# Masks of the first attention scores: from TensorE products to a fused VectorE add-and-maximum

## The reference, cut to what matters

```python
h = shift_token(x)
q, k, v = split(h @ wqkv)                      # 8 heads of 64
q, k = rotary_xpos(l2norm(q) * qs, l2norm(k) * ksc)
sim = einsum('bhwid,bhwjd->bhwij', bq, bk)     # windows of 128 queries, 256 keys
mask = (i < j) | (i > j + WINDOW) | (j == -1)
sim = where(mask, -finfo.max, sim)
attn = softmax(sim, axis=-1)
x = x + (attn @ bv) @ wo
h = layernorm(shift_token(x)) * lg + lb
a, g = split(h @ w1 + b1)
x = x + (a * gelu(g)) @ w2 + b2
```

## Time and profile before

| | us |
|---|---|
| median of 3 runs | 4159.85 (4159.74 to 4161.44) |
| profiled execution, its own time | 4161.62 |
| its span | 4159.9 |
| busy: PE, PEld | 3578.2, 2115.6 |
| busy: DVE | 2682.2 |
| busy: ACT | 2142.1 |
| busy: POOL | 1476.1 |
| mean granted TensorE clock | 0.946 |

### The profile page before, as it was taken

The page is one execution under the profiler, slowest core; times in us unless marked ns, Lnnn a source line. Parts: engine busy times, 40 slices in busy tenths (PEclk is TensorE's granted clock), DMA queues, the critical chain, the costliest instruction groups (busy, mean ns, idle before and its releaser), DMA issues.

```text
span 4159.9 us, 74766 instructions
## 1 busy us (share of the span) xinstructions
PE 3578.2 (86%) x26976; PEld 2115.6 (51%) x26976; DVE 2682.2 (64%) x4386; ACT 2142.1 (51%) x2586; POOL 1476.1 (35%) x1468
## 2 busy tenths in 40 slices
PE   2778788778775689999999999948899999999999
PEld 1222222222222456766676667625576667666666
DVE  4767667677673467667766776535766776676664
ACT  1555545555553345555555555424455555555564
POOL 1100101101001434544454555223454455445543
PEclk7999989999997789999999999978999999999999
DMA  2221211222212000110011001120011001100101
GB/s 48 36 47 41 48 36 40 52 41 38 45 36 68 6 21 23 33 34 24 23 33 35 23 23 37 32 68 14 14 33 35 23 23 33 35 23 30 36 21 34
DMA packets 149353, 139.79 MB, mean 34 GB/s; under 512 B 11420, under 2 KB 147664, under 8 KB 149200
## 3 DMA queue, kind: packets, MB, share of 16 engines
q1 hardware_dynamic: 149200, 137.78, 13.2%
HBM read 70.40 MB, written 33.55 MB: 25 GB/s over the span
## 4 chain that ended last, share of the span: by engine, by line
issue 35%; POOL 24%; PE 7%; DVE 2%; POOLq 1%; ACT 0%; DVEq 0%; ACTq 0%
POOL f_u L1392 6%; POOL f_u L1397 5%; POOL f_hT_l L1408 4%; POOL f_Pl L1416 3%; POOL f_xb L1424 2%; POOL f_Pl L1418 2%; PE f_p L946 1%; PE f_p L1027 1%; PE f_p L1068 1%; PE f_p L1046 1%; POOL f_mark_l L1413 1%; POOL f_qst L1402 1%; DVE f_negm L1278 0%; POOLq L1412 0%; PE f_p L963 0%
## 5 line engine op out<-in xcount | busy, mean ns | idle before, releaser
L646 DVE TENSOR_REDUCE m_negm<-m_p 128x2 f16<-128x1024 f32 x512 | 605.3, 1221 | 246.5 <-PE m_p L465 206.1
L565 ACT ACTIVATE m_Pr<-m_p 128x1024 f32<-128x1024 f32 x512 | 492.8, 1018 | 268.4 <-PE m_p L483 267.9
L1392 POOL TENSOR_TENSOR f_u<-f_u,f_bt 128x1024 f32<-128x1024 f32 x128 | 302.0, 2359 | 622.5 <-DVE f_bt L1250 622.5
L1027 PE MATMUL f_p<-f_vl,f_Pl 128*128 128x65 f32 x3584 | 430.3, 280 | 14.4 <-POOL f_Pl L1418 14.4
L1027 PEld LDWEIGHTS f_p<-f_vl,f_Pl 128*128 128x128 f32 x3584 | 418.8, 196 | 25.4 <-issue 24.7
L685 POOL TENSOR_TENSOR m_rc<-m_rc,m_rs 128x1024 f32<-128x1024 f32 x32 | 75.5, 2358 | 979.1 <-DVE m_rs L641 977.6
L1149 ACT ACTIVATE f_Pl<-f_p 128x896 f32<-128x896 f32 x256 | 220.4, 914 | 329.5 <-PE f_p L1013 220.1
L492 PE MATMUL m_o<-m_Pr,m_vm 128*32 128x512 f32 x2048 | 369.7, 678 | 17.3 <-ACT m_Pr L565 16.8
L1408 POOL TENSOR_TENSOR f_hT_l<-f_hp,f_hT_h 128x512 f16<-128x512 f32 x192 | 221.7, 1155 | 406.4 <-ACT f_hp L1172 405.3
L946 PE MATMUL f_p<-f_wq_h,f_xT_h 128*128 128x512 f16 x768 | 296.4, 386 | 76.1 <-DVE f_mark_x L1236 47.9
L1164 ACT ACTIVATE f_G<-f_p,f_bias 128x512 f32<-128x512 f32 x192 | 131.4, 684 | 344.2 <-PE f_p L1068 344.2
(11 more groups left out here) (217 smaller groups left out, 7892.6 us busy)
## 6 DMA issues: line engine op xcount, KB each, us to landing
f_xs<-out SPq DMA_DIRECT2D x32, 512.0 KB, 4.8
f_xr<-out SPq DMA_DIRECT2D x32, 512.0 KB, 4.5
f_xh<-attn_res SPq DMA_DIRECT2D x32, 512.0 KB, 3.9
out<-f_xb SPq DMA_DIRECT2D x32, 512.0 KB, 3.2
m_xin<-in_L_attn_x SPq DMA_DIRECT2D x16, 512.0 KB, 4.3
m_QT<-m_hi SPq DMA_DIRECT2D x128, 64.0 KB
m_KT<-m_hi SPq DMA_DIRECT2D x128, 64.0 KB
out<-m_xn SPq DMA_DIRECT2D x16, 512.0 KB, 6.6
```

The source lines that it names most:

```text
L565: act.activation(Pr[kt % 2][:, 2 * u:2 * u + 2, :].rearrange("p h t -> p (h t)"), psum[w.slot("M2", g, kt, u)][:, :], ACT.Exp).then_inc(*w ...
L646: dve.tensor_reduce(negm[:, t, pr // 2, :, pr % 2], psum[w.slot("M1", h, u)][:, :].rearrange("p (a k) -> p a k", a=2), AX.X, ALU.max, nega ...
L1027: mm = pe.matmul(psum[w.slot("PV", hp)][:, e * T + t * (DH + 1):e * T + (t + 1) * (DH + 1)], Pl[h % 4][:, at * W:(at + 1) * W], vl[:, j, h ...
L1392: pool.tensor_tensor(u[t][:], u[t][:], bt[:], ALU.add).then_inc(*bt_used.up(I))
```

## The change

The masks leave TensorE. `l1` of TensorE no longer writes them, the score products start their own sums, and the first window's empty half is not written at all. `l1` of VectorE replaces the one reduction over 1024 columns by four fused instructions for each head, one for each window: each adds the mask (now f32 in SBUF) to 256 scores in PSUM (128 in the first window), writes the sum back to the same place in PSUM, and puts the row's maximum into `tops`. A one-element memset stands in front of the four. The copy in `lm` turns the sign. A mask matrix less is made at the start.

The lists of steps change too. On TensorE `F.W1,3` now stands ahead of `C.L1,3`. On VectorE `A.RN` and `F.W1,3` stand ahead of `C.L1,3` and `C.LM`, all `A.SH` steps stand at the end, and `C.OT,1` and `C.WO,0` ahead of `N.XH`. On GpSimd `A.QK,3` stands behind `F.H1,2`. On ScalarE and SyncE some steps change places.

```diff
         "PE": """...
-               F.W1,2 C.L1,2 C.L1,3 F.W1,3 F.W1,4 F.W1,5 C.LM F.W2,0 ...
+               F.W1,2 C.L1,2 F.W1,3 C.L1,3 F.W1,4 F.W1,5 C.LM F.W2,0 ...
         "ACT": """...
-               F.H1,1 F.W1,3 F.H1,2 F.W1,4 F.H1,3 F.W1,5 C.LM F.H1,4 F.H1,5 A.HI,0 ... C.L2,3 C.OT,0 A.HI,1 N.XH
-               C.OT,1 A.HI,2 A.HI,3""",
+               F.H1,1 F.W1,3 F.H1,2 F.W1,4 F.H1,3 C.LM F.W1,5 F.H1,4 F.H1,5 A.HI,0 ... C.L2,3 A.HI,1 C.OT,0 C.OT,1
+               N.XH A.HI,2 A.HI,3""",
-        "DVE": """... F.W1,0 F.W1,1 C.L1,0 C.L1,1 F.W1,2 C.L1,2 C.L1,3 C.LM A.RN F.W1,3 F.W1,4 F.W1,5
-               F.W2,0 N.LN F.W2,1 F.W2,2 A.SH,0 C.PV,0 C.PV,1 C.PV,2 C.OT,0 C.PV,3 N.XH C.OT,1 C.WO,0 C.WO,1 C.WO,2 C.WO,3 A.SH,1
-               A.SH,2 N.ZB A.SH,3""",
-        "POOL": """A.QK,0 A.QK,1 A.QK,2 A.QK,3 F.H1,0 F.H1,1 F.H1,2 A.NM,0 F.H1,3 ... N.LS A.SQ,1 ...
-        "SP": """F.W2,0 A.XT N.LX F.W2,1 F.W2,2 C.XR N.XH""",
+        "DVE": """... F.W1,0 F.W1,1 C.L1,0 C.L1,1 F.W1,2 C.L1,2 A.RN F.W1,3 C.L1,3 C.LM F.W1,4 F.W1,5 N.LN
+               F.W2,0 F.W2,1 F.W2,2 C.PV,0 C.PV,1 C.PV,2 C.OT,0 C.PV,3 C.OT,1 C.WO,0 N.XH C.WO,1 C.WO,2 C.WO,3 A.SH,0 A.SH,1 A.SH,2
+               A.SH,3 N.ZB""",
+        "POOL": """A.QK,0 A.QK,1 A.QK,2 F.H1,0 F.H1,1 F.H1,2 A.QK,3 A.NM,0 F.H1,3 ... A.SQ,1 N.LS ...
+        "SP": """A.XT N.LX F.W2,0 F.W2,1 F.W2,2 C.XR N.XH""",
...
-        masks, mask0, sel = sb("masks", [P, 2, P], BF16), sb("mask0", [P, 2, P], BF16), sb("sel", [P, H, P], BF16)
+        masks, sel = sb("masks", [P, 2, P], F32), sb("sel", [P, H, P], BF16)
...
@@ tensor, l1
-                for n in range(NT):
-                    for ps in tiles:
-                        pe.matmul(ps[:, 2 * n * W:2 * (n + 1) * W], identb[:],
-                                  (mask0 if n == 0 else masks)[:].rearrange("p a k -> p (a k)"),
-                                  start=True, stop=False, skip_group_check=True)
...
-                                       KH[half, 2 * hp + e, (n - 1 + lo) * W:(n + 1) * W], start=False, stop=True, skip_group_check=True)
+                                       KH[half, 2 * hp + e, (n - 1 + lo) * W:(n + 1) * W], start=(n % 2 == 0), stop=True, skip_group_check=True)
@@ vector, l1 and lm
                     dve.wait_ge(*w.is_full("L1", h))
-                    dve.tensor_reduce(negm[:, :, h], psum[w.slot("L1", h)][:, :].rearrange("p (n k) -> p n k", n=NT),
-                                      AX.X, ALU.max, negate=True).then_inc(*w.frees("L1", h))
+                    dve.memset(mark_t[:, h:h + 1], 0.0)
+                    for n in range(NT):
+                        lo = 1 if n == 0 else 0
+                        ins = dve.tensor_tensor_reduce(out=psum[w.slot("L1", h)][:, (2 * n + lo) * W:2 * (n + 1) * W],
+                                                       in0=psum[w.slot("L1", h)][:, (2 * n + lo) * W:2 * (n + 1) * W],
+                                                       in1=masks[:, lo:2, :].rearrange("p a k -> p (a k)"), scale=1.0, scalar=MASKED,
+                                                       op0=ALU.add, op1=ALU.max, accum_out=tops[:, n, h:h + 1])
+                    ins.then_inc(*w.frees("L1", h))
...
-                dve.tensor_copy(negm4[:, :, :, 0:H], negm[:].unsqueeze(2).to_broadcast([P, NT, P // G32, H])).then_inc(*negm_ready.up(I))
+                dve.tensor_scalar(negm4[:, :, :, 0:H], tops[:].unsqueeze(2).to_broadcast([P, NT, P // G32, H]), -1.0, None, ALU.mult).then_inc(*negm_ready.up(I))
```

More of the change, by code:

```diff
@@ L766, in layers_phase @@
         "PE": """C.V,0 C.V,1 C.V,2 C.V,3 A.XT C.ST,0 A.QK,0 C.ST,1 A.QK,1 C.ST,2 A.QK,2 C.ST,3 A.QK,3 F.W1,0 F.W1,1 C.L1,0 C.L1,1
-               F.W1,2 C.L1,2 C.L1,3 F.W1,3 F.W1,4 F.W1,5 C.LM F.W2,0 C.L2,0 F.W2,1 F.W2,2 C.L2,1 C.PV,0 C.L2,2 C.L2,3 C.PV,1 C.PV,2
+               F.W1,2 C.L1,2 F.W1,3 C.L1,3 F.W1,4 F.W1,5 C.LM F.W2,0 C.L2,0 F.W2,1 F.W2,2 C.L2,1 C.PV,0 C.L2,2 C.L2,3 C.PV,1 C.PV,2
                C.OT,0 C.PV,3 N.XH C.OT,1 C.WO,0 C.WO,1 C.WO,2 C.WO,3""",
         "ACT": """C.V,0 C.V,1 C.V,2 C.V,3 A.XT C.ST,0 A.QK,0 C.ST,1 A.QK,1 C.ST,2 A.QK,2 C.ST,3 A.QK,3 F.W1,0 F.W1,1 F.H1,0 F.W1,2
-               F.H1,1 F.W1,3 F.H1,2 F.W1,4 F.H1,3 F.W1,5 C.LM F.H1,4 F.H1,5 A.HI,0 C.L2,0 C.L2,1 C.L2,2 C.L2,3 C.OT,0 A.HI,1 N.XH
-               C.OT,1 A.HI,2 A.HI,3""",
-        "DVE": """A.XT A.QK,0 A.QK,1 A.QK,2 A.QK,3 F.W1,0 F.W1,1 C.L1,0 C.L1,1 F.W1,2 C.L1,2 C.L1,3 C.LM A.RN F.W1,3 F.W1,4 F.W1,5
-               F.W2,0 N.LN F.W2,1 F.W2,2 A.SH,0 C.PV,0 C.PV,1 C.PV,2 C.OT,0 C.PV,3 N.XH C.OT,1 C.WO,0 C.WO,1 C.WO,2 C.WO,3 A.SH,1
-               A.SH,2 N.ZB A.SH,3""",
-        "POOL": """A.QK,0 A.QK,1 A.QK,2 A.QK,3 F.H1,0 F.H1,1 F.H1,2 A.NM,0 F.H1,3 F.H1,4 F.H1,5 A.SQ,0 C.L2,0 C.L2,1 A.NM,1 C.L2,2 C.L2,3
-               N.LS A.SQ,1 A.NM,2 A.SQ,2 A.NM,3 A.SQ,3""",
-        "SP": """F.W2,0 A.XT N.LX F.W2,1 F.W2,2 C.XR N.XH""",
+               F.H1,1 F.W1,3 F.H1,2 F.W1,4 F.H1,3 C.LM F.W1,5 F.H1,4 F.H1,5 A.HI,0 C.L2,0 C.L2,1 C.L2,2 C.L2,3 A.HI,1 C.OT,0 C.OT,1
+               N.XH A.HI,2 A.HI,3""",
+        "DVE": """A.XT A.QK,0 A.QK,1 A.QK,2 A.QK,3 F.W1,0 F.W1,1 C.L1,0 C.L1,1 F.W1,2 C.L1,2 A.RN F.W1,3 C.L1,3 C.LM F.W1,4 F.W1,5 N.LN
+               F.W2,0 F.W2,1 F.W2,2 C.PV,0 C.PV,1 C.PV,2 C.OT,0 C.PV,3 C.OT,1 C.WO,0 N.XH C.WO,1 C.WO,2 C.WO,3 A.SH,0 A.SH,1 A.SH,2
+               A.SH,3 N.ZB""",
+        "POOL": """A.QK,0 A.QK,1 A.QK,2 F.H1,0 F.H1,1 F.H1,2 A.QK,3 A.NM,0 F.H1,3 F.H1,4 F.H1,5 A.SQ,0 C.L2,0 C.L2,1 A.NM,1 C.L2,2 C.L2,3
+               A.SQ,1 N.LS A.NM,2 A.SQ,2 A.NM,3 A.SQ,3""",
+        "SP": """A.XT N.LX F.W2,0 F.W2,1 F.W2,2 C.XR N.XH""",
     }
@@ L840, in layers_phase @@
         vl = sb("vl", [P, NT, H, DH + 1], F32)
-        negm, negm4, mT = sb("negm", [P, NT, H], BF16), sb("negm4", [P, NT, P // G32, G32], BF16), sb("mT", [P, T], BF16)
+        tops, negm4, mT = sb("tops", [P, NT, H], F32), sb("negm4", [P, NT, P // G32, G32], BF16), sb("mT", [P, T], BF16)
         Pall = sb("Pl", [P, 4, NK], F32)
@@ L855, in layers_phase @@
         mark_l, mark_a = sb("mark_l", [1, H], F32), sb("mark_a", [1, 1], F32)
+        mark_t = sb("mark_t", [1, H], F32)
         mark_x, mark_h = sb("mark_x", [1, 1], F32), sb("mark_h", [1, 1], F32)
@@ L878, in layers_phase @@
         const_done, mask_zero, mask_done = [ctx.enter_context(nc.semaphore("f_" + n)) for n in ("const_done", "mask_zero", "mask_done")]
-        N_CONST, N_MASK = 7, 12
+        N_CONST, N_MASK = 7, 10
         out_v = out.rearrange("b (t p) d -> b p t d", p=P)
@@ L1368, in _ @@
             w = Walk(ph, pool, "POOL", B)
-            mats = (ident, identb, identf, sel, masks, mask0)
+            mats = (ident, identb, identf, sel, masks)
             for m in mats:
@@ L1383, in _ @@
                                pattern=[[1, P]], channel_multiplier=-1).then_inc(mask_done, 1)
-            pool.memset(mask0[:, 0, :], MASKED).then_inc(mask_done, 1)
-            for m in (masks, mask0):
+            for m in (masks,):
                 pool.affine_select(out=m[:, 1, :], in_=m[:, 1, :], compare_op=ALU.is_ge, fill=MASKED, base=0,
```

## The result

The changed kernel takes 4301.29 us (median of four, 4298.18 to 4311.4) where the kernel before takes 4159.8 (four, 4158.63 to 4161.44): 1.0342 times as long, 95% interval 1.0329 to 1.0354. The prediction was 4303. The profiled execution took 4311.4, its span is 4309.7, and its mean granted clock 0.920, where it was 0.946. Of the kernel called half and half further down, one execution of six, three times as long as the others, is left out of every figure.

The account below looks back on a forecast made before the run. It took the round as bound by TensorE, with VectorE also full from F.W1,0 to C.L2,0. 26 rounds x 4.8 = 125 us, plus 20, minus 2, made +143: 4305 profiled, 4303 median; range 4190 to 4390.

Parts of the forecast that it names:

- The masks' 3.92 us turned into waits: TensorE's mask products, four steps a round: their removal gains nothing in the stretch, as TensorE waits for VectorE instead.
- C = 1.55 us a head: VectorE's time for one head's maxima with the fused instructions, 1.155 before; ends 1.29 and 1.82; 3.2 us more a round.
- RN held: VectorE's RN, now ahead of C.L1,3, stands still under two GpSimd instructions and loses 1.15 + 2.37 = 3.5 us.
- The rival's thought: Rival, RN isn't held: the lock could pass between two GpSimd instructions; a round loses 3.5 us less, 4212; chance 0.13.
- The rival of the falling clock: TensorE's clock falls after the wait before W1,5; C.LM 1.8 us later, 4350; chance 0.22 together with the dear instruction.
- The round: From one F.W1,0 to the next: 8C - 7.6 = 4.8 us longer, times 26 rounds 125 us.
- The sections without F: Second and third of both layers: 5 us each for dearer heads and RN ahead of C.LM, 20 in all.
- The other sections: The two last sections have no RN and C.LM starts some 1 us earlier: -2 us.
- The rival of the dear instruction: Fused instruction at C = 1.82: a round 7.0 us longer, 4366; chance 0.22 together with the falling clock.

Follow-up runs that it names:

- half and half: Changed kernel with mended lists, but heads 0 to 3 with TensorE's masks and plain reductions, heads 4 to 7 fused: 4096.42 us, 0.9839 of the kernel before.
- mended lists: Changed kernel's lists with A.RN behind C.PV,0, A.QK,3 early, GpSimd's C.L2 steps ahead of spare work: fused for all heads 4117.33 us, for heads 0 to 3 4125.18.
- the lists alone: Kernel before with the changed kernel's lists of steps, masks still by TensorE, one reduction a head: 4241.69 us, 1.0201 of the kernel before.

## Why the prediction was right

The round got longer by the mechanism forecast. The sizes were off in both directions, and a part of the agreement is luck.

- *The masks' 3.92 us turned into waits.* Right, and shown by itself: taken away at no price they are worth 0.56 us a round.
- *C = 1.55 us a head.* It is 1.40, inside the ends. The fixed part of a fused instruction is 0.12 us (0.38 less 256 columns of 1.02 ns, the slope from 0.25 and 0.38), close to the 0.13 taken from L1351; the memset, costed at 0.09, lies nearly whole inside the instruction beside it. 8 x 0.15 = 1.2 us a round less than forecast. The Trainium skill (VectorE: DVE Perf Modes, The TRN2 errata) had given 1.53; this trace is below it.
- *RN held.* Right in place and cause. Its start, with C = 1.40, comes out as 7.47 + 6 x 1.40 = 15.9 us after F.W1,0; measured 15.75 in the short round. It lasts 6.0 us, 3.1 unheld, so the hold is 2.9 and not 3.5. The forecast took GpSimd's two durations whole, 1.15 + 2.37; but the first held instruction starts 0.20 us into L1409, and each of the two does its own 0.23 us of work within the hold, so they lose 0.83 and 2.03. 0.6 less. The rule of the Trainium skill (SBUF — State Buffer, Who interferes with whom) that the second engine to issue is fully blocked agrees with L246's 2.26 us under GpSimd's 2.33. The rival's thought, that VectorE gets in between two instructions of GpSimd, was true of L245 and helped no further: the next, L246, was held by the next. L1338's 6.57 us under five in a row show that it isn't always true.
- *The rival of the falling clock was true at the same time, and the sum left it out.* After the wait of 3.85 us TensorE is granted 0.61 or 0.51 in W1,5, so mostly 1.2 of its 2.4 GHz. In the short round the copy of the maxima (L1285) ends at 2197.05, and C.LM starts at 2198.41 and not before, 1.4 us late, as its products stand behind W1,5. In the long round W1,5 makes it 2.2 us late (2284.46 to 2286.62), and all up to there is 1.2 us late already, by W1,2 at half pace: 3.4. With 10 short and 14 long rounds that is 2.5 us on average. The rival had priced W1,5 alone, at 1.8, and no sentence of the forecast has the clock falling at W1,2.
- *The round.* 4.8 - 1.2 - 0.6 + 2.5 = 5.5; measured 87.42 - 82.02 = 5.4, times 26 is 140 us, where 125 were forecast.
- *The sections without F.* Forecast 20 us for the second and third of both layers, measured +1.6 and +0.1, +0.3 and +1.6: 4 us. The 20 was the term worst sized; the other end, 0 if GpSimd's chain hides it, was nearer. No run shows what hides it.
- *The other sections.* The two last were forecast at -2; with the thirteenth rounds ahead of them they are 5 us longer than a round's growth explains. The two first are 2 shorter, where nothing was forecast.
- *Not in the forecast:* 2.8 us in the stretch ahead of the layers, whose instructions the change doesn't touch. The first mark of the layers comes anywhere from 1320.6 to 1334.7 us in the thirteen traces, so this is scatter.
- *A slip.* The rival of the dear instruction comes to 4160 + 208 = 4368, not 4366.

The sum with measured sizes is 140 + 4 + 5 - 2 + 3 = 150, and the profiled execution is 150 us longer: 4311.4, 6 above the 4305 of the forecast. So 65 us of clock (26 x 2.5) that the sum hadn't got were met by 31, 16 and 16 us that it had too much for the fused instruction, the hold and the sections without F. That they cancel is luck, and so is that the median, which moved by 141, lies within 2 us of 4303.

What stays open: what makes the clock fall at W1,2, as in more than half of the rounds. The instructions are the same in both sorts, and so are the waits up to W1,2 (0.25, 0.88 and 0.74 us in that round, 0.26, 0.88 and 0.74 in the short one). Every long round of the kernel with A.QK,3 moved, and of the mended lists with the fused form for heads 0 to 3 or for all, has the same fall at W1,2, and no short one has it. No run here changed the clock alone.

## What to carry to other kernels

Ask of each stretch which engine's list ends it; TensorE was the busiest at 86%, and taking 3.3 us of work a round from it gave 0.56. Work handed to the engine that is second busiest comes back as a wait, and a wait can come back a second time through the granted clock of the products behind it: the single waits before W1,5 did so at 3.85 us in all of 24 rounds, at 2.4 us in 23 of 24, and at 1.8 us in none. Before a small SBUF instruction of VectorE is moved, list the GpSimd instructions that run without a gap from its new place on, since the sum of their durations may be what it costs; and where two forms of one step load two engines differently, try the mix, with the form that is quick on the waited-for engine first.

## What the runs showed of the hardware

- The fused add-and-maximum with a PSUM input and output starts every 0.38 us over 256 columns and 0.25 over 128, though the profile gives it 0.47 and 0.29 to 0.33, and each has a record of its own of 0.14 us (DVE_READ_ACCUMULATOR2_ANT) that lies beside the next. Its price is read from start to start.
- It isn't held by GpSimd, though its mask is in SBUF: the head beside L1409 took 1.36 us.
- A VectorE instruction on SBUF alone that comes under a run of GpSimd instructions may be let in between two of them (L245, 1.06 us, between L1409 and L1393) or be held through the whole run (L1338 of 128 columns, 6.57 us). What decides it is open.
- The clock can make one and the same round alternate: 86.2 and 88.2 us after the change, 80.6 and 81.8 in the fused kernel with mended lists. With the lists alone the same wait of 2.4 us is followed by a full clock once (83.8 us) and by a fallen one 23 times (85.3 to 85.5).
